# A gated cross-attention stack: second buffers in the local attention, text attention and ternary layer as one pipeline, and one ScalarE step moved in the last attention

## What is computed

```python
x = x + tanh(g_xattn[0]) * L0_xattn(layernorm(x), ctx)   # local attention over channels, window 16
x = x + tanh(g_ffn[0])   * L0_ffn(layernorm(x))          # mixture of low-rank experts
x = x + tanh(g_xattn[1]) * L1_xattn(layernorm(x), ctx)   # 32 heads, 4 key heads
x = x + tanh(g_ffn[1])   * L1_ffn(layernorm(x))
x = x + tanh(g_xattn[2]) * L2_xattn(layernorm(x), ctx)   # text attention, one head of 512
x = x + tanh(g_ffn[2])   * L2_ffn(layernorm(x))          # ternary layer
x = x + tanh(g_xattn[3]) * L3_xattn(layernorm(x), ctx)   # 32 heads, 8 key heads, rms norm of q and k
x = x + tanh(g_ffn[3])   * L3_ffn(layernorm(x))
```

```python
def L0_xattn(x, cond):            # per channel pair: q, k, v = W x + b; scores over a window of 16 columns
    dots = einsum('bhdt,bhdtw->bhtw', qh, k_win) * hd ** -0.5
    out = einsum('bhtw,bhdtw->bhdt', softmax(dots), v_win)
    return Wo @ out + bo
def L2_xattn(text, features):
    Q, K = text @ Wq.T + bq, features @ Wk.T + bk
    return softmax(Q @ K.T / sqrt(512)) @ features
def L2_ffn(x):                    # ternary layer
    xn = rms_norm(x)
    xq = clip(round(xn * s), -128, 127) / s          # s = 127 / max|xn| of the row
    wq = clip(round(W / mean|W|), -1, 1) * mean|W|
    return x + gelu(xq @ wq.T + b)
def L3_xattn(x, c):               # rms norm of every q and k head, then attention, then Wo
    return softmax(rmsnorm(q) @ rmsnorm(k).T / sqrt(128)) @ v @ Wo.T
```

## Time and profile before

| | us |
|---|---|
| median of 3 runs | 3844.86 |
| lowest and highest run | 3837.51, 3853.58 |
| the profiled execution, its time | 3847.08 |
| its span in the trace | 3845.3 |

### The profile page before, as it was taken

The page is one execution under the profiler, slowest core; times in us unless marked ns, Lnnn a source line. Parts: engine busy times, 40 slices in busy tenths (PEclk is TensorE's granted clock), DMA queues, the critical chain, the costliest instruction groups (busy, mean ns, idle before and its releaser), DMA issues. The chain is left out here.

```text
span 3845.3 us, 49596 instructions
## 1 busy us (share of the span) xinstructions
PE 3421.7 (89%) x17944; PEld 2754.6 (72%) x17954; DVE 1862.5 (48%) x3717; ACT 1493.3 (39%) x3346; POOL 938.8 (24%) x515
## 2 busy tenths in 40 slices
PE   6999998799899989979988944999899899989996
PEld 5777775588678778868864732778587767857784
DVE  4677765243434433433344456455455545545554
ACT  3334432244344334434432433444344334434442
POOL 1111102232233232323322302222222232222220
PEclk8899998899999999999998977999999999999998
DMA  2000000221022021112101101221112121112111
GB/s 92 1 1 1 1 1 20 88 67 59 26 83 69 30 84 63 49 56 72 63 28 77 44 3 52 86 63 41 68 60 63 35 72 61 55 42 65 63 38 50
DMA packets 57161, 191.32 MB, mean 50 GB/s; under 512 B 9152, under 2 KB 9920, under 8 KB 53184
## 3 DMA queue, kind: packets, MB, share of 16 engines
q1 hardware_dynamic: 57024, 189.46, 14.7%
HBM read 185.24 MB, written 4.19 MB: 49 GB/s over the span
## 5 line engine op out<-in xcount | busy, mean ns | idle before, releaser
L1515 POOL TENSOR_TENSOR h_wql<-h_rq,h_wqh 128x1024 fp32r<-128x1024 f32 x112 | 277.2, 2475 | 919.2 <-ACT h_wqh L1539 919.2
L1802 DVE TENSOR_TENSOR h_ol<-ps,h_oh 128x512 fp32r<-128x512 f32 x256 | 177.1, 692 | 652.4 <-ACT h_oh L1586 652.4
L131 PE MATMUL ps<-h_woh,h_oh 128*128 128x512 f32 x1024 | 437.0, 427 | 22.2 <-DVE h_ol L1802 22.0
L133 PE MATMUL ps<-h_woh,h_ol 128*128 128x512 f32 x1024 | 405.0, 396 | 0.0
L132 PE MATMUL ps<-h_wol,h_oh 128*128 128x512 f32 x1024 | 403.9, 394 | 0.0
L1519 POOL TENSOR_TENSOR h_wol<-h_ro,h_woh 128x1024 fp32r<-128x1024 f32 x128 | 306.4, 2394 | 186.7 <-ACT h_woh L1544 186.7
L1586 ACT CAST h_oh<-ps 128x512 fp32r<-128x512 f32 x256 | 149.4, 584 | 439.6 <-PE ps L1690 439.6
L1798 DVE COPY h_tf<-ps 128x512 f32<-128x512 f32 (+1 forms) x256 | 142.5, 557 | 312.4 <-PE ps L1682 312.2
L1690 PE MATMUL ps<-h_tf,h_vf 128*128 128x128 f32 x2048 | 274.0, 277 | 6.3 <-DVE h_tf L1798 4.0
L1690 PEld LDWEIGHTS ps<-h_tf,h_vf 128*128 128x128 f32 x2048 | 258.3, 191 | 26.2 <-DVE h_tf L1798 15.7
L1612 ACT ACTIVATE h_ex<-ps,h_mx 128x128 f32<-128x128 f32 x512 | 180.9, 365 | 240.8 <-DVE h_mx L1831 240.8
(11 more groups left out here) (279 smaller groups left out, 6936.6 us busy)
## 6 DMA issues: line engine op xcount, KB each, us to landing
h_rq<-in_L_Wq SPq DMA_DIRECT2D x128, 512.0 KB, 3.6
h_ro<-in_L_Wo SPq DMA_DIRECT2D x128, 512.0 KB, 3.9
h_rk<-in_L_Wk SPq DMA_DIRECT2D x48, 256.0 KB, 2.7
h_craw<-in_ctxT SPq DMA_DIRECT2D x10, 1024.0 KB, 5.4
cnat<-in_ctx SPq DMA_DIRECT2D x4, 1024.0 KB, 11.5
t_craw<-in_ctxT SPq DMA_DIRECT2D x4, 1024.0 KB, 5.1
t_cn<-in_ctx SPq DMA_DIRECT2D x4, 1024.0 KB, 6.0
out_rows<-x SPq DMA_DIRECT2D x16, 256.0 KB, 2.0
```

Source lines behind the costliest of these rows:

```text
L131: nc.tensor.matmul(dst, lh, rh, start=start, stop=False, **kw)
L133: return nc.tensor.matmul(dst, ll, rh, start=False, stop=stop, **kw)
L1515: nc.gpsimd.tensor_tensor(wql[:, par], rq[:, par], f(wqh[:, par]), ALU.subtract).then_inc(m["p_wq"], 1)
L1802: nc.vector.tensor_tensor(by_head(ol), ps[:, AB, :].rearrange("p (b h t) -> p b h t", h=2, t=S), f(by_head(oh)), ALU.subtract).then_inc(m[ ...
```

## The change

It has three parts.

**Local attention.** `qx`, `kp` and `vx` get a second buffer, chosen by j % 2. The writers of tile j + 1 wait for the last quarter of tile j - 1. POOL writes all eight heads of `qx`, and DVE's `queries` and its semaphore `v_qx` go. On PE `queries` and `keys` of the next tile stand behind `scores` of n = 0, `values_of_context` behind that of n = 1, `value_rows` behind that of n = 2, and `output` of the last tile behind that of n = 3, where it waits for `a_vx` of the next tile, since both use bank PB. ACT's copies move with them, and `values_out` of the next tile comes at n = 2. The statistics of the next group are cut into single tiles on DVE.

**Text and ternary.** One phase does both, and the ternary layer of group g - 1 runs inside step g of the text attention. Queries, keys and values keep two PSUM banks, 4 and 5, and the ternary products take 6 and 7. A product of the queries or keys may now start only when ACT has copied the one two before it. The rows for the quantizer are now written normed twice by one ACT instruction for each tile; the 16 squares with their accumulator reads (L1041) go. DVE rounds the ternary weights in place of POOL. POOL gets `keep`, which applies one multiply and add to each tile of x. The raw ternary weights load into the buffer of the raw key weights, after these were split.

**Last attention.** ACT takes `queries_square(n + 1)` ahead of `out_high(n)`.

```diff
-                qx = sb("qx", [P, D // TB, HEADS0, TB], ctx=ph)
+                qx = sb("qx", [P, 2, D // TB, HEADS0, TB], ctx=ph)
-                kp = sb("kp", [P, 2, PADT], ctx=ph)
+                kp = sb("kp", [P, 2, 2, PADT], ctx=ph)
-                vx = sb("vx", [P, 8, 2, 4, S], ctx=ph)
+                vx = sb("vx", [P, 2, 8, 2, 4, S], ctx=ph)
...
-                            wait(pool, s_s, NQ * j)
-                            for h in range(HEADS0 // 2):
+                            wait(pool, s_s, NQ * (j - 1))
+                            for h in range(HEADS0):
...
                         def output(j):
                             pe.wait_ge(a_o, j + 1)
+                            pe.wait_ge(a_vx, min(j + 3, NTILE))
...
-                            wait(act, s_s, NQ * j)
+                            wait(act, s_s, NQ * (j - 1))
...
-                            wait(act, s_av, NQ * j)
+                            wait(act, s_av, NQ * (j - 1))
...
                                 powers(g)
-                                if n == 0:
-                                    values_out(j)
+                                if n == 0 and j + 1 < NTILE:
+                                    queries_out(j + 1)
+                                    keys_out(j + 1)
                                 if n == 1:
                                     if j:
                                         picked(j - 1)
                                     if j + 1 < NTILE:
-                                        row(j + 1)
+                                        context_values_out(j + 1)
                                 if n == 2 and j + 1 < NTILE:
-                                    queries_out(j + 1)
-                                if n == 3 and j + 1 < NTILE:
-                                    keys_out(j + 1)
-                                    context_values_out(j + 1)
+                                    values_out(j + 1)
...
+                        def keep(g):
+
+                            for i in tiles(g):
+                                j = i % NT
+                                pool.wait_ge(q_xn, i + 1)
+                                nc.gpsimd.tensor_scalar(x[:, i], x[:, i], qs[:, 4, j:j + 1], qs[:, 5, j:j + 1],
+                                                        ALU.mult, ALU.add).then_inc(q_xp, 1)
...
-                            out(g, s_q, a_q, qt, bq2)
-                            if more:
-                                rows(g + 1)
+                            out(g, (0, 1), s_q, a_q, qt, bq2)
+                            if g > 1:
+                                gelus(g - 2)
+                            out(g, (2, 3), s_q, a_q, qt, bq2)
+                            if g:
+                                ternary_rows(g - 1)
                             act.wait_ge(v_m, g + 1)
                             nc.scalar.activation(ex[:], sc[:], ACT.Exp, scale=SCALE).then_inc(a_e, 1)
                             if more:
-                                out(g + 1, s_k, a_k, kt, bk2)
+                                rows(g + 1)
+                                out(g + 1, range(NC), s_k, a_k, kt, bk2)
                                 high(g + 1)
+                            if g:
+                                quants_out(g - 1)
...
                             if g + 1 < G:
                                 turn(g + 1)
+                            if g:
+                                if g == 1:
+                                    pe.wait_ge(v_tern, 1)
+                                turn_quants(g - 1)
                             values(g)
+                            if g:
+                                ternary(g - 1)
+                        turn_quants(G - 1)
+                        ternary(G - 1)
...
                                 split_steps(act, i, t, last, kv, q, o)
+                                if norm and not (last and t == NS - 1):
+                                    queries_square(n + 1)
                                 if not (first and t == 0):
                                     out_high(n)
                                 if norm and not (last and t == NS - 1):
-                                    queries_square(n + 1)
                                     queries_root(n + 1, (t + 1) % 2)
```

More of the change, by code:

```diff
@@ L902, in turn @@
                         def turn(g):
-                            for i in range(NT * g, NT * g + NT):
+                            for i in tiles(g):
                                 pe.wait_ge(a_xn, i + 1)
@@ new lines, in linear_out @@
+                        def linear_out(g):
+                            for i in tiles(g):
+                                j = i % NT
+                                dve.wait_ge(q_sy, i + 1)
+                                wait(dve, q_vx, i - NT + 1)
+                                nc.vector.scalar_tensor_tensor(out=y[:, j], in0=ps[:, 6 + i % 2, :], scalar=qs[:, 2, j:j + 1],
+                                                               in1=bf2[:], op0=ALU.mult, op1=ALU.add).then_inc(q_vy, 1)
```

434 lines of the change are left out of this document (218 added, 216 removed).

## The result

| | before | after |
|---|---|---|
| median of 4 runs | 3848.09 us | 3713.20 us |
| lowest and highest run | 3837.51, 3853.58 | 3705.63, 3716.66 |
| span of the profiled execution | 3845.3 us | 3714.5 us |

The changed kernel takes 0.965 of the time of the kernel before, with a 95% interval of 0.9622 to 0.9678. The forecast was 3710 us, 3 us beside the median. Two of its terms were off by more than 10 us, in opposite directions, so that the sum came closer than its parts is luck.

What follows compares the result with a forecast made beforehand. PE was taken to bound the local, text and last attention, but not the ternary phase. Savings of 67.5 + 35 + 32 = 134.5 us gave 3712.6 from the profiled execution, 3710 us against the median, range 3670 to 3770.

Steps and rivals of the forecast that it cites:

- Gaps of the local attention: Local attention: PE's waits mostly go, a tile takes 28.0 us instead of 30.8, saving 42 us over 15 tiles.
- The start: Local attention: the first scores wait for eight heads by POOL in place of four, costing 4.5 us.
- The clock: Local attention: the lowered clock costs about 46 us; most falls go with the gaps, giving 30 us back.
- Rival 1: Local attention: the clock gives nothing back, falls may come from light products; 3740 us, chance 0.17.
- One more stretched instruction, inside DVE's slack, so nothing: Local attention: POOL's longer work stretches one more DVE instruction a tile, 0.6 us, at no cost in time.
- Rival 4: Local attention: POOL's heads slow DVE until it bounds the tile at 30.8 us; 3782 us, chance 0.05.
- Text and ternary: Joint phase: steps 1 and 2 take 44 us each, tail 35 us, 7 us taken off for the clock; saves 35 us.
- Last attention: Last attention: the moved square removes PE's waits for it, less a new wait in the key step; saves 32 us.
- the step that leaves 1.0 us a head: Last attention: 1.8 us gained less about 0.8 us of new wait, for 8 heads in 4 groups.
- Rival 2: Whole kernel: all works, clock back in full, tile 27.8 us, text steps 39 us; 3661 us, chance 0.10.
- Rival 3: Joint phase and last attention: text steps at 50 us, key step takes back all but 10 us; 3752 us, chance 0.10.
- Rival 5: Local attention: PE runs at 1.2 GHz throughout, making the kernel slower than before; 4028 us, chance 0.03.

Runs made afterwards that it cites:

- The filled kernel: The kernel before, with short products nobody reads placed in PE's pauses in the local attention: 3801.81 us, ratio 0.9898.
- The kernel with all edits: The changed kernel with Newton steps, output product, three joint-phase steps, the keys' square and the copy of the new keys moved: 3645.70 us, ratio 0.9474.

## Why the prediction was right, point by point

- **Gaps of the local attention (42 us): right.** 27.76 us for a tile where 28.0 was said, and the output product's wait is 0.36 us where 0.5 was said:

```profile
286.22 1.10 PE L346 MATMUL ps<-oc,bd_o 128*128 128x512 f32 x2 [0.36 <-ACT vx L411]
```

That is 3.04 us for each of 12 tiles. In the three with the Newton steps it is 1.13, from 30.8 to the 29.67 at full clock. Together it is 40 us.

- **The start (+4.5 us): wrong, it cost nothing.** The first scores start at 33.62 us, and 33.59 before. The step took POOL's time as if nothing hid it. But PE reaches the scores only behind the context values and their transposes. Before, these ended at 33.80 by the trace, 3.6 us after POOL's four heads (25.61 + 4.58, at 30.19). The other four heads add 3.4 us, not 4.5, so POOL's eight end at 33.57, just when the scores start. PE's timeline before:

```profile
31.83 1.97 PE L283 MATMUL ps<-ident,vw 128*128 128x128 f32 x8 [1.49 <-ACT vw L391]
```

POOL's timeline after, and PE's:

```profile
25.55 8.02 POOL L263 TENSOR_TENSOR qx<-qs,hmask 128x512 f32<-128x512 f32 x8 [13.99 <-ACT qs L385]
```

```profile
31.32 1.09 PE L293 MATMUL ps<-ident,vw 128*128 128x128 f32 x8 [1.49 <-ACT vw L403]
33.62 3.62 PE L303 MATMUL ps<-kp,qx 128*128 128x64 f32 x16 [1.20 <-POOL qx L263]
```

- **The clock (30 of 46 us): right in kind, low in size.** 80.4 - 40 leaves 40 us, though two tiles still fall to the lower level for a while. The filled kernel shows 43 to 50 us for nearly all of it (0.98), and the two falls that are left cost 6.6 us each (36.30 - 29.67). Rival 1 falls.
- **"One more stretched instruction, inside DVE's slack, so nothing": wrong.** It holds for the common tile, where two or three two-input instructions are stretched. Once in four tiles three small ones stand there and lose 2.4 us together, and through the exponential, `vx` and the output product that becomes a wait of PE and a fall of the clock. Moving them gave 17 us against the mean of the changed order. Rival 4 had the mechanism but asked whether DVE bounds the tile. The right question was which instruction stands beside POOL's eight and who is queued behind it.
- **Text and ternary (35 us): right, with errors that cancel.** Steps 1 and 2 took 87.7 us together, where 88 was said, but as 46.05 and 41.64. PE's wait for `t_xl` was 2.98 us in step 1 (row below), at the low end of 3 to 5, and 1.06 in step 2, which has no statistics of a later group. The last softmax came 26.9 us later than before, where 25 was said. In the last step the values and transposes waited for DVE, which made the way from the softmax to the end of the attention's additions 21.4 us in place of 13.4, and this the forecast did not have. The tail behind it was 31 us where 35 was said. The 7 us that were set aside for the clock cover the rest: 26.9 + 8.0 + 31 is 66 us, and 25 + 35 + 7 is 67.

```profile
2121.14 1.23 PE L972 MATMUL ps<-ident,t_xn 128*128 128x128 f32 x8 [2.98 <-DVE t_xl L1057]
```

- **Last attention (32 us): the term was too large by 13 us.** The wait for h_sq went as said, and the one for h_ksq came as said, 0.62 us where 0.8 was expected. What failed is the step that leaves 1.0 us a head: it counted one pause for the key step, and missed POOL. Casts by ACT and low parts by POOL stand in a chain behind the exponential, and PE, now earlier, waits for its end. It costs 0.47 us a head, so 0.73 was left of 1.0. And the step counted 8 heads in a group: the first distance between two h_wkl of a group (46.6 to 47.8 us before, 47.6 to 48.0 after) did not shrink, and a group became 4.6 us shorter, not 8. With both waits gone, last attention and last mixture together take 56 us less, more than the 48 that the forecast had as the most for this square.
- **Rival 2** (all works, 3661 us) was given 0.10. The kernel with all edits goes below it, but with seven more edits than the change had. **Rival 3** (3752 us) fell: steps of 46.05 and 41.64 us are far from 50, and the moved square kept 19 us, not 10. **Rival 4** fell too, since PE is busy 27.40 of 27.76 us in a tile and DVE 22.44. **Rival 5** fell, since the clock rose with less idle time.

## What to carry to other kernels

- Where TensorE is full and its clock is below 1.00, put products that nobody reads into the pauses. It is a cheap test of what the pauses cost beyond their own length, here 43 to 50 us of clock beside 45 us of gaps (3.0 us in each of 15 tiles), and it can be left in if the pauses can't be closed.
- Before work moves to GpSimd, list the DVE instructions that will stand beside it, the small ones too, and follow the wait from each of them to the engine that is full.
- When a wait is removed in a loop, everything that is timed by the slow chain (here the exponential) comes closer to being late. Look at the idle time ahead of each product in the trace: what had a few tenths to spare is next.

## What the runs showed that was not expected

- An instruction of DVE on 128x4 numbers took 0.96 to 0.99 us beside POOL, six times its 0.16, while one on 128x512 numbers went from 0.69 to 1.10 or 1.20. The small one lost 0.8 us and the large one 0.4 to 0.5. The loss does not shrink with the instruction, so many small ones in a row are the worst to have there.
- 138 added products of 128 columns made the kernel 39 us faster.
- The table load ahead of the gelus took 1.28 us. The Trainium skill gives about 2.66 us for a switch, with a drain behind the load ("ScalarE: Activation LUTs", What ACT_TABLE_LOAD costs). In the tail of the changed kernel the load at 2237.07 ends at 2238.35, and the gelu starts at 2238.96, when DVE's result is there. No drain shows.
